# Linear attention laid over chunks: a five-stage order in place of a loop of four passes

## The chip, the cores and the metric

One core of one Trainium2 chip runs the whole kernel in one launch. The engines are TensorE (PE in the rows, PEld its weight loads), VectorE (DVE), ScalarE (ACT), GpSimd (POOL) and SyncE (SP), which issues the DMAs. The metric is the device time of the launch in microseconds, as the median of several runs.

## The reference, cut to what matters

Input x is 4 x 512 tokens of 512 features. It passes four blocks: a linear attention with residual, a routed spline lookup, a differential softmax attention, and a gated feed-forward with Hadamard-mixed weights; the kernel runs the lookup, a norm and the feed-forward around both attentions. The change concerns the part up to the end of the linear attention and its routing:

```python
q = (x @ Wq.T + bq), k = (x @ Wk.T + bk), v = (x @ Wv.T + bv)   # 16 query heads, 8 key heads of 32
q = q * cos + rotate_half(q) * sin                              # the same for k
x = x / max(norm(x), 1e-6); p = x @ R.T                         # per head, R is 16 x 32
feats = concat(sin(p), cos(p)) / sqrt(32)
kv = einsum('bhsf,bhsd->bsfd', kp, v); out = einsum('bhsf,bsfd->bhsd', qp, kv)   # per token, over heads
return out @ Wo.T + bo
# routed lookup: layernorm, signs, scores of 64 tiles, argmax (cluster, then tile),
# min and max of the chosen 8 features over all tokens of a tile, 16-cell piecewise lookup, added to x
```

## The kernel before

The 2048 tokens are four chunks of 512 (NCH = 4), each chunk four tiles of 128 (TPC). Products in 16 bits are made as three (high by high, high by low, low by high: `pairs_product`, L1189), so a 512 x 512 by 128 product is 12 matmuls. TensorE writes PSUM, eight banks of 512 floats (`k.ps`); ScalarE and VectorE take results out. The engines run their own instruction lists and meet through semaphores; on every engine the order is that of the code.

Set-up (`setup_*`, L596 to L954) loads and transposes the weights, mixes the feed-forward weights, and routes all chunks once. Its load order is in `setup_sync`: Wq, x, Wk and Wv, Wo, the four parts of W_down, then eight groups of up and gate weights. Then, for chunk 0, the lookup is applied and its rows are normalized and transposed (L957 to L1169), and the linear attention starts.

A pass `b_*(i, last, next)` (L1209 to L1486) does for chunk i: four value products (taken out at L1411, sent to DRAM and back in another layout by SP, L1380 and L1383); six projections into banks 2 and 3 (L1318), each rotated by a matmul (L1229), multiplied by cosines on GpSimd (L1368) and by sines on VectorE (L1421, L1422), squared on GpSimd (L1372) and summed per head by a matmul (L1234). The inverse lengths come from a square root (L1333) and a reciprocal with one refinement step (L350 to L353). Six products with the random matrix (L1258) are scaled by the spread inverse lengths (L1261, L1330, L1439), reduced to a turn (L1445, L1447), put through Sin (L1340) and split into high and low (L1343, L1451). SP spreads these over 36 transfers (L1391) into `ks` and `qs`. Then 16 pairs of 16-token groups: scores (L1277), mask (L1460), weighted values (L1287), results (L1354, L1485); four output products (L1297), residual (L1475) and bias (L1478). Into the projections of chunk i the routing of chunk i-1 is woven (`last`), between angles and pairs the lookup of chunk i+1 (`next`, L1266 and L1454), and after the pairs its addition, statistics, Sqrt (L1140), rows (L1148) and transposes (L1167). Chunks 1 and 2 run in a hardware loop (`Fori`, L2490), 0 and 3 are written out. After the last chunk its routing stands alone (L2493), then the tile ranges are joined and the lookup and feed-forward phase begins, with its own norm through Ln and Exp (`norm_root_scalar`, L1723).

## Time and profile before

| | us |
|---|---|
| median of 3 runs | 2496.23 (2494.53 to 2498.5) |
| the profiled execution | 2493.57 |
| its span, first to last instruction | 2491.8 |
| TensorE busy | 2077.4 (83%) |
| VectorE busy | 1250.5 (50%) |
| ScalarE busy | 743.3 (30%) |
| GpSimd busy | 200.6 (8%) |

The page cuts the span into 40 slices of 62.3 us and gives the busy share of each engine in tenths, and under PEclk the clock that TensorE was granted, in tenths of full speed (1.0 is 2.4 GHz, 0.5 is 1.2 GHz). A table by stretches gives for each the busy time and instruction count of every engine; a timeline gives instructions in order, with the idle time before them and what ended it in brackets. Matmuls overlap each other, so a mean duration of one is longer than its share of a row of many.

### The profile page before, as it was taken

Reading aid. Unit: us, or ns where it says so; the run is one execution under the profiler, and the core shown is the slowest. Engines: PE = TensorE matmul, PEld = TensorE weight load, DVE = VectorE, ACT = ScalarE, POOL = GpSimd, SP = SyncE. Lnnn points to the kernel's source line nnn. Section 1 sums busy time; section 2 is a strip of 40 time slices with the busy share of each in tenths; the row PEclk is TensorE's granted clock in tenths of the full one; section 3 lists DMA queues with packets and bytes.
Section 4 is the critical chain, followed back from the end, with each engine's and each line's share of the span. In section 5 each row is a group of like instructions: output and inputs, shape, how many; then the busy total and the mean of one; then the engine's idle time right before and its main releaser. Section 6 shows DMA issues by size and latency. Waiting matters only on the chain. (4 is left out here: it accounts for less than half of the span.)

```text
span 2491.8 us, 30544 instructions
## 1 busy us (share of the span) xinstructions
PE 2077.4 (83%) x12014; PEld 981.1 (39%) x12014; DVE 1250.5 (50%) x2301; ACT 743.3 (30%) x1146; POOL 200.6 (8%) x148
## 2 busy tenths in 40 slices
PE   4777477756658548999999999999999999999998
PEld 3444224223223224444444444444444444444443
DVE  4444456364464444645456625662567355633332
ACT  4443131223212312222323522352235223521211
POOL 3340010101002000000000101000100010000000
PEclk8777577767678668999999999999999999999999
DMA  6211420111001311222210211121112111222322
GB/s 255 68 51 17 167 37 22 7 39 17 23 16 17 106 69 62 97 96 85 77 43 29 77 56 35 34 77 51 42 35 77 51 43 34 71 74 100 104 99 87
DMA packets 90978, 158.70 MB, mean 64 GB/s; under 512 B 44182, under 2 KB 55772, under 8 KB 86108
## 3 DMA queue, kind: packets, MB, share of 16 engines
q1 hardware_dynamic: 90844, 156.86, 19.6%
q8 instruction: 91, 1.49, 0.2%
q14 instruction: 43, 0.35, 0.1%
HBM read 128.52 MB, written 18.87 MB: 59 GB/s over the span
## 5 line engine op out<-in xcount | busy, mean ns | idle before, releaser
L1189 PE MATMUL ps<-arena 128*128 128x512 f16 (+1 forms) x4512 | 1006.6, 379 | 30.5 <-DVE arena L1675 12.8
L1189 PEld LDWEIGHTS ps<-arena 128*128 128x128 f16 x4512 | 436.2, 99 | 533.4 <-issue 29.6
L1620 PE MATMUL ps<-arena 128*128 128x512 f16 x1536 | 347.8, 382 | 29.4 <-DVE arena L1666 16.2
L1620 PEld LDWEIGHTS ps<-arena 128*128 128x128 f16 x1536 | 147.2, 98 | 206.7 <-issue 28.1
L1642 ACT ACTIVATE arena<-ps,arena 128x512 f32<-128x512 f32 x128 | 87.7, 685 | 362.4 <-PE ps L1189 362.1
L1675 DVE SCALAR_TENSOR_TENSOR arena<-arena,ps 128x512 f32<-128x512 f32 x128 | 87.8, 686 | 210.2 <-ACT arena L1642 209.5
L2229 ACT ACTIVATE arena<-ps 128x1024 f32<-128x1024 f32 (+3 forms) x128 | 90.2, 705 | 251.9 <-PE ps L2138 251.9
L2334 DVE CAST arena<-arena 128x1024 f16<-128x1024 f32 (+3 forms) x128 | 66.6, 520 | 148.1 <-ACT arena L2229 146.1
L2300 DVE TENSOR_REDUCE arena<-ps 128x2 f32<-128x256 f32 (+3 forms) x128 | 99.5, 819 | 65.1 <-PE ps L2082 65.1
L1684 DVE SCALAR_TENSOR_TENSOR arena<-ps,arena 128x512 f32<-128x512 f32 x128 | 95.7, 748 | 39.8 <-PE ps L1189 39.8
L1703 DVE SCALAR_TENSOR_TENSOR arena<-ps,arena 128x512 f32<-128x512 f32 x64 | 44.0, 687 | 139.7 <-PE ps L1620 139.5
L2336 DVE TENSOR_TENSOR arena<-arena 128x1024 f16<-128x1024 f32 (+3 forms) x128 | 111.4, 870 | 4.4
L2280 POOL TENSOR_TENSOR arena<-arena 128x512 f16<-128x512 f32 x32 | 37.1, 1159 | 742.1 <-ACT arena L2207 742.1
L1666 DVE TENSOR_TENSOR arena<-arena 128x512 f16<-128x512 f32 x128 | 91.6, 715 | 4.0 <-ACT arena L1634 4.0
L1634 ACT ACTIVATE arena<-arena 128x512 f16<-128x512 f32 x128 | 79.7, 622 | 17.5 <-DVE arena L1684 17.5
L685 PE MATMUL ps<-arena 128*128 128x128 f32 x240 | 44.9, 347 | 46.5 <-DVE arena L917 27.5
L728 PE MATMUL ps<-arena 128*128 128x512 f16 x256 | 71.9, 450 | 5.7 <-DVE arena L917 5.7
L1277 PE MATMUL ps<-arena 96*128 96x256 f16 x128 | 29.2, 323 | 54.2 <-issue 32.0
L2136 PE MATMUL ps<-arena 32*128 32x512 f16 (+3 forms) x768 | 72.9, 293 | 0.0
L2204 ACT ACTIVATE arena<-ps 128x512 f32<-128x512 f32 x32 | 19.1, 597 | 166.7 <-PE ps L1189 166.7
L1460 DVE TENSOR_TENSOR arena<-ps,arena 128x256 f32<-128x256 f32 x128 | 47.3, 418 | 38.7 <-PE ps L1277 36.3
L2284 POOL TENSOR_TENSOR arena<-arena 128x512 f32<-128x512 f32 x16 | 18.6, 1163 | 580.2 <-DVE arena L2347 580.2
(266 smaller groups left out, 2442.5 us busy)
## 6 DMA issues: line engine op xcount, KB each, us to landing
arena<-wug_dram SPq DMA_DIRECT2D x128, 512.0 KB, 3.3
arena<-wd_hi_dram SPq DMA_DIRECT2D x16, 1024.0 KB, 5.0
arena<-wd_lo_dram SPq DMA_DIRECT2D x16, 1024.0 KB, 7.2
arena<-arena SPq DMA_DIRECT2D x144, 64.0 KB, 2.1
wug_dram<-arena SPq DMA_DIRECT2D x4, 2048.0 KB, 15.8
arena<-_attn_hidden_states_dram SPq DMA_DIRECT2D x4, 1024.0 KB, 10.4
arena<-in_L_ffn_W_down_dram SPq DMA_DIRECT2D x4, 1024.0 KB, 15.5
arena<-in_L_ffn_W_up_dram SPq DMA_DIRECT2D x8, 512.0 KB, 6.3
```

Of the source, the lines that this page charges most:

```text
L728: ins = pe.matmul(k.ps[:, bank, :], sign, part[:, jc, :], start=(n == 0), stop=(n == 7))
L1189: ins = pe.matmul(out, left[a](c), right[b](c), start=(at == 0), stop=(at == 3 * n - 1))
L1620: ins = pe.matmul(k.ps[:, bank, :], act[x][:, slot, cols], wd[y][:, f, :], start=(f == 0 and m == 0), stop=(f == 7 and m == 2))
L1634: e.activation(k.act_hi[:, g % ACT_SLOTS, :], k.prod[:, g % 2, :], ACT.Copy).then_inc(s["f_hi"], 1)
L1642: e.activation(k.th[:, g % 2, :], k.ps[:, GATE_BANK, :], ACT.Tanh, scale=k.wscale[:, FB + a:FB + a + 1])\
L1666: e.tensor_tensor(k.act_lo[:, g % ACT_SLOTS, :], k.prod[:, g % 2, :], k.act_hi[:, g % ACT_SLOTS, :], ALU.subtract)\
L1675: e.scalar_tensor_tensor(out=th, in0=th, scalar=1.0, in1=k.ps[:, GATE_BANK, :], op0=ALU.add, op1=ALU.mult)\
L1684: e.scalar_tensor_tensor(out=k.prod[:, g % 2, :], in0=k.ps[:, UP_HALF_BANK, :], scalar=k.wscale[:, a:a + 1], in1=th, op0=ALU.mult, op1=ALU ...
L2136: pe.matmul(k.ps[:, bank, queries], x[rows, 4 + b, keys], y[rows, b, queries], start=False, stop=False)
L2229: e.activation(k.p32[:, t % 2, :, queries], k.ps[:, 0:2, queries], ACT.Exp, scale=SCORE).then_inc(s["c_exp"], 1)
L2300: e.tensor_reduce(k.mx[:, u, 4 * b + 2 * j:4 * b + 2 * j + 2], k.ps[:, bank:bank + 2, 0:(u + 1) * P], AXX, ALU.max).then_inc(s["c_max"], 1)
L2336: e.tensor_tensor(k.p_lo[:, t % 2, :, queries], k.p32[:, t % 2, :, queries], k.p_hi[:, t % 2, :, queries], ALU.subtract).then_inc(s["c_p_l ...
```

## The change

The passes become stages -1 to 3, all written out; the hardware loop is gone. In stage i the roles are `now` = i, `new` = i+1, `look` = i+2 and `back` = i-1, where they exist. A stage begins with 17 steps: at step y the scores of pair y and the weighted values of pair y-1 of chunk `now`, and at fixed steps a projection, a rotation or a length of chunk `new` (`QK_AT` = 1, 2, 4, 5, 7, 8; `ROT_AT` = 3, 4, 6, 7, 9, 10; `LENGTH_AT` = 5, 6, 8, 9, 11, 12). On VectorE the token statistics of `back` stand at steps 0, 2 and 4, and the range update of chunk i-2 at step 1. Then the angles of `new` alternate with the output rows of `now` and the lookup of `look`; then the values of `new`, the routing of `back` and the normalization and transposes of `look`. In stage 3 the routing of chunk 2 is in the 17 steps instead.

The bias of the output is added on GpSimd. Square roots with reciprocals become Ln, Exp with factor -0.5, and the same refinement step (`root_refine_vector`), for the lengths, the routing's two deviations and the norm. One bank serves all rotations (4), another all spreads; the lookup's rows are written as cells, slopes and bases into three banks. The buffers of the attention move into the space of the feed-forward weights, after their copy to DRAM is done. SP issues the spread transfers of a chunk first and its values' round trip after them. In the set-up Wk and Wv are loaded before x and taken first, and W_down's parts are loaded one after each of the first four groups. The later lookups read their rows as two halves, by two instructions.

```diff
...
+    k.q2, a = v.at(a, [P, 2, CH], F32)
     k.qr, a = v.at(a, [P, 6, CH], F32)
-    k.q2, a = v.at(a, [P, 2, CH], F32)
-    k.y2, _ = v.at(a, [P, TPC, HID], F32)
-    k.ks, a = v.at(a, [P, 8, CH], F16)
-    k.masked2, _ = v.at(a, [P, 2048], F32)
-    k.ksg, _ = v.at(a, [P, 32, P], F16)
+    k.f_hi, a = v.at(a, [P, 6, CH], F16)
+    k.f_lo, a = v.at(a, [P, 6, CH], F16)
     k.ang, a = v.at(a, [P, 2, CH], F32)
     k.turns, a = v.at(a, [P, 2, CH], F32)
...
+    b = k.wug_at
+    k.qs, b = v.at(b, [P, 16, CH], F16)
+    k.ks, b = v.at(b, [P, 8, CH], F16)
+    k.ksg, b = v.at(b, [P, 32, P], F16)
+    k.ot_hi, b = v.at(b, [P, KC, CH], F16)
+    k.ot_lo, b = v.at(b, [P, KC, CH], F16)
+    k.sm, b = v.at(b, [P, 2, 2, 16, 16], F32)
     k.vr, b = v.at(b, [P, 32, 32], F32)
+    k.y2, b = v.at(b, [P, TPC, HID], F32)
+    k.v0, b = v.at(b, [P, TPC, 256], F32)
...
+def token_root_scalar(k, e, i, n):
+    s = k.s
+    ve, out = k.t4[0], k.t4[1 if n == 1 else 4]
+    done = s["std1" if n == 1 else "std2"]
+    e.wait_ge(s["var1" if n == 1 else "var2"], i + 1)
+    e.activation(out, ve, ACT.Ln).then_inc(done, 1)
+    e.wait_ge(done, 2 * i + 1)
+    e.activation(out, out, ACT.Exp, scale=-0.5).then_inc(done, 1)
...
+    load_nat(1, [(rows_of(d["L0_attn_Wk"]), 2), (rows_of(d["L0_attn_Wv"]), 2)])
     for c in range(NCH):
         sp.dma_start(k.x[:, c * TPC:(c + 1) * TPC, :],
                      d["L0_attn_hidden_states"][c].rearrange("(u p) n -> p u n", p=P)).then_inc(s[f"x_in{c}"], 16)
-    load_nat(1, [(rows_of(d["L0_attn_Wk"]), 2), (rows_of(d["L0_attn_Wv"]), 2)])
     load_nat(2, [(rows_of(d["L0_attn_Wo"])[:, 0:2], 2), (rows_of(d["L0_attn_Wo"])[:, 2:4], 2)])
...
+        if g < 4:
+            sp.dma_start(k.wd_nat[:, g, :], d["L1_ffn_W_down"][g * P:(g + 1) * P, :]).then_inc(s[f"wd_in{g}"], 16)
...
     first(0)
+    first(1)
     setup_stats_vector(k, V)
     setup_scale_vector(k, V)
-    first(1)
+    first(2)
     setup_norm_vector(k, V)
-    first(2)
...
+def b_roles(i):
+    return [n if 0 <= n < NCH else None for n in (i, i + 1, i + 2, i - 1)]
...
+    for bank, n, at in ((LOOK_CELLS, 3, 256), (LOOK_SLOPES, P, 128), (LOOK_BASES, P, 0)):
+        for u in range(TPC):
+            ins = pe.matmul(k.ps[:, bank, u * n:(u + 1) * n], k.oht[:, u * P:(u + 1) * P], k.table[:, at:at + n],
+                            start=True, stop=True)
...
+        if now is not None:
+            if y < PAIRS:
+                score(y)
+            if y:
+                weighted(y - 1)
+        if new is not None:
+            if y in QK_AT:
+                project(QK_AT.index(y))
+            if y in ROT_AT:
+                rotate(ROT_AT.index(y))
+            if y in LENGTH_AT:
+                length(LENGTH_AT.index(y))
...
+    body = back is not None and new is not None
+    if look is not None:
+        pe.wait_ge(s["b_n2"], new + 1)
+        apply_turn_tensor(k, pe, look, 1, LOOK_CELLS)
+    turns(0)
+    output(0)
+    if look is not None:
+        look_rows_tensor(k, pe, look)
+    turns(1)
+    output(1)
+    turns(2)
+    output(2)
+    turns(3)
+    output(3)
+    turns(4)
+    value(0)
+    turns(5)
+    value(1)
+    if body:
+        if look is not None:
+            pe.wait_ge(s["ap_read"], look + 1)
+        route_turn_tensor(k, pe, back, route, 0, BACK_BANK)
+        route_turn_tensor(k, pe, back, route, 1, BACK_BANK)
+    value(2)
+    if body:
+        route_turn_tensor(k, pe, back, route, 2, BACK_BANK)
+        route_turn_tensor(k, pe, back, route, 3, BACK_BANK)
+    value(3)
+    if body:
+        route_key_tensor(k, pe, back, route, BACK_KEY)
+    if look is not None:
+        pe.wait_ge(s["b_spread"], 6 * (new + 1))
+        pe.wait_ge(s["b_y"], 6 * (new + 1))
+        for c in range(KC):
+            if c == 3:
+                pe.wait_ge(s["n_lo"], 2 + KC * look + 1)
+            turn_tensor(k, pe, look, c, NEXT_TURN[c])
+    if body:
+        route_hot_tensor(k, pe, back, route, BACK_BANK[0])
+        for c in range(KC):
+            route_mask_tensor(k, pe, back, route, c, BACK_BANK)
+        route_slice_tensor(k, pe, back, route, BACK_KEY)
...
+    if look is not None:
+        apply_scalar(k, e, look, 1, LOOK_CELLS)
+    for z in range(4):
+        turns(z)
+    keys(0)
+    keys(1)
+    turns(4)
+    keys(2)
+    keys(3)
+    turns(5)
+    if body:
+        route_sign_scalar(k, e, back, route, 0, BACK_BANK)
+        route_sign_scalar(k, e, back, route, 1, BACK_BANK)
+    if body:
+        route_sign_scalar(k, e, back, route, 2, BACK_BANK)
+        route_sign_scalar(k, e, back, route, 3, BACK_BANK)
+    if look is not None:
+        use_log(e)
+        norm_root_scalar(k, e, look)
+        norm_write_scalar(k, e, look, look, k.h, range(TPC), s["n_h"])
+        for c in range(KC):
+            turn_scalar(k, e, look, c, NEXT_TURN[c])
+    if body:
+        route_hot_scalar(k, e, back, route, BACK_BANK[0])
...
+    if now is not None:
+        for u in range(TPC):
+            e.wait_ge(s["b_res"], TPC * now + u + 1)
+            xt = k.x[:, now * TPC + u, :]
+            e.tensor_tensor(xt, xt, k.bo, ALU.add).then_inc(s["b_bo"], 1)
...
+    for y in range(PAIRS + 1):
+        if now is not None:
+            if y < PAIRS:
+                mask(y)
+            if y % 4 == 1 and y > 4:
+                sums(y // 4 - 1)
+        if i >= 2 and y == 1:
+            route_ends_vector(k, V, i - 2, route, BACK_KEY)
+        if new is not None:
+            if y - 1 in ROT_AT:
+                rope(ROT_AT.index(y - 1))
+            if y == SPREAD_AT:
+                lengths()
+            if y == REFINE_AT:
+                refine()
+        if look is not None and y == PAIRS:
+            spline_start_vector(k, V, look)
+        if back is not None:
+            if y == 0:
+                token_sums_vector(k, V, back)
+            if y == 2:
+                token_first_vector(k, V, back)
+            if y == 4:
+                token_second_vector(k, V, back)
+        if i == NCH - 1:
+            if y == 10:
+                route_choice_vector(k, V, back, route, LAST_KEY)
+            if y in (12, 13):
+                route_pick_vector(k, V, back, route, 2 * y - 24, LAST_BANK)
+                route_pick_vector(k, V, back, route, 2 * y - 23, LAST_BANK)
+    body = back is not None and new is not None
+    if now is not None:
+        sums(3)
+    angle(0)
+    if look is not None:
+        spline_place_vector(k, V, look, 1, cells)
+    residual(0)
+    low(0)
+    angle(1)
+    if look is not None:
+        spline_slope_vector(k, V, slopes)
+    residual(1)
+    low(1)
+    angle(2)
+    if look is not None:
+        spline_value_vector(k, V, bases)
+    residual(2)
+    low(2)
+    angle(3)
+    if look is not None:
+        scale_start_vector(k, V, look)
+        scale_tiles_vector(k, V, look, range(TPC))
+    residual(3)
+    low(3)
+    angle(4)
+    value(0)
+    if look is not None:
+        for u in range(TPC):
+            scatter_tile_vector(k, V, u)
+    low(4)
+    angle(5)
+    value(1)
+    if look is not None:
+        add_sum_vector(k, V, look)
+    low(5)
+    if look is not None:
+        norm_sums_vector(k, V, look, range(TPC))
+        norm_spread_vector(k, V)
+    value(2)
+    if look is not None:
+        norm_refine_vector(k, V, look)
+    value(3)
+    if body:
+        route_choice_vector(k, V, back, route, BACK_KEY)
+    if look is not None:
+        for c in range(KC):
+            turn_vector(k, e, look, c, NEXT_TURN[c])
+    if body:
+        for c in range(KC):
+            route_pick_vector(k, V, back, route, c, BACK_BANK)
+    if i == NCH - 1:
+        route_ends_vector(k, V, back, route, LAST_KEY)
...
```

## Rows read from the trace of the kernel before

**Rows 1.** The page, 40 equal slices: TensorE busy and granted clock, in tenths.
```profile
PE   4777477756658548999999999999999999999998
PEclk8777577767678668999999999999999999999999
```
**Rows 2.** Stretches of the span: length, then busy time and count by engine, clock, DMA.
```profile
core 0: us, PE busy (x) PEld busy (x) DVE busy (x) ACT busy (x) POOL busy (x), PEclk, DMA share, GB/s
0.00:265.90 265.90, 181.51 (x843) 111.01 (x843) 117.20 (x237) 110.34 (x171) 74.76 (x36) 0.78 0.31 101
...
300.10:432.40 132.30, 98.12 (x594) 47.00 (x595) 74.12 (x150) 30.78 (x45) 12.58 (x12) 0.78 0.15 29
432.40:596.30 163.90, 101.89 (x610) 48.07 (x609) 83.53 (x181) 39.90 (x61) 12.64 (x12) 0.73 0.11 22
596.30:756.40 160.10, 101.93 (x609) 48.06 (x608) 83.47 (x181) 39.87 (x60) 12.62 (x12) 0.73 0.12 22
756.40:880.80 124.40, 83.24 (x520) 34.57 (x518) 58.20 (x120) 33.89 (x50) 12.62 (x12) 0.75 0.23 59
880.80:915.80 35.00, 16.25 (x78) 11.96 (x78) 12.43 (x42) 9.25 (x15) 0.00 (x0) 0.60 0.00 0
```
**Rows 3.** The same view of the steps of the second pass.
```profile
432.40:473.40 41.00, 31.65 (x128) 11.77 (x126) 14.76 (x38) 13.26 (x21) 12.64 (x12) 0.89 0.19 18
473.40:484.90 11.50, 9.96 (x43) 6.01 (x42) 3.87 (x10) 0.00 (x0) 0.00 (x0) 0.80 0.00 0
484.90:494.60 9.70, 1.94 (x2) 0.50 (x2) 6.06 (x5) 0.63 (x1) 0.00 (x0) 0.50 0.00 0
494.60:516.40 21.80, 11.98 (x13) 3.15 (x12) 14.52 (x25) 12.42 (x19) 0.00 (x0) 0.50 0.17 43
516.40:533.20 16.80, 4.82 (x12) 3.03 (x12) 6.63 (x23) 4.38 (x5) 0.00 (x0) 0.50 0.35 86
533.20:554.60 21.40, 16.39 (x288) 8.49 (x288) 14.55 (x37) 2.39 (x4) 0.00 (x0) 0.85 0.01 2
554.60:565.20 10.60, 10.52 (x48) 4.57 (x48) 9.51 (x15) 0.00 (x0) 0.00 (x0) 1.00 0.01 2
565.20:585.50 20.30, 3.88 (x16) 3.14 (x16) 9.76 (x23) 6.81 (x10) 0.00 (x0) 0.63 0.00 1
```
**Rows 4.** Timeline of the set-up: start, length, engine, line, and idle time before.
```profile
41.52 0.45 PE L685 MATMUL ps<-arena 128*128 128x128 f32 x1 [6.53 <-DMA arena<-in_L_ffn_W_up_dram]
```
**Rows 5.** Timeline of the second pass: a projection at full clock and a rotation.
```profile
460.14 2.76 PE L1189 MATMUL ps<-arena 128*128 128x512 f16 x12
...
462.73 1.02 PE L1229 MATMUL ps<-arena 128*128 128x512 f32 x2
```
**Rows 6.** Groups by line in the second pass: busy, mean ns of one | idle before.
```profile
L1460 DVE TENSOR_TENSOR arena<-ps,arena 128x256 f32<-128x256 f32 x32 | 12.0, 419 | 6.3 <-PE ps L1277 5.2 <-issue 0.5
...
L1439 DVE SCALAR_TENSOR_TENSOR arena<-ps,arena 128x512 f32<-128x512 f32 x6 | 4.1, 685 | 5.2 <-ACT arena L1330 5.2
...
L350 DVE RECIPROCAL arena<-arena 24x512 f32<-24x512 f32 x1 | 3.3, 3341 | 0.9 <-ACT arena L1333 0.9
...
L1445 DVE TENSOR_SCALAR arena<-arena 128x512 f32<-128x512 f32 x6 | 2.9, 487 | 1.3 <-DVE arena L1439 1.2
...
L1478 DVE TENSOR_TENSOR arena<-arena 128x512 f32 x4 | 2.8, 692 | 0.6
```
**Rows 7.** Stretches before the first pass: lookup, addition, statistics to transposes.
```profile
271.90:279.10 7.20, 0.00 (x0) 0.00 (x0) 6.38 (x21) 0.00 (x0) 0.00 (x0) 0.50 1.02 419
279.10:286.50 7.40, 0.00 (x0) 0.00 (x0) 7.21 (x12) 0.00 (x0) 0.00 (x0) 0.50 0.65 265
286.50:300.10 13.60, 3.94 (x16) 3.13 (x16) 6.79 (x19) 5.52 (x9) 0.00 (x0) 0.50 0.00 1
```
**Rows 8.** Timeline of the last routing: the slice of the chosen features.
```profile
904.49 6.99 PE L468 MATMUL ps<-arena 128*128 128x8 f32 x32 [0.78 <-DVE arena L506]
```
**Rows 9.** Timeline of SP's queue in the second pass: the spread transfers.
```profile
506.33 23.30 SPq L1391 DMA_DIRECT2D arena<-arena  x36
```
**Rows 10.** Timeline: the same small VectorE operation beside GpSimd and alone.
```profile
433.28 1.09 POOL L1368 TENSOR_TENSOR arena<-arena 128x512 f32<-128x512 f32 x1 [96.01 <-ACT arena L1318]
433.33 1.08 DVE L374 TENSOR_SCALAR arena<-arena 128x4 f32<-128x4 f32 x1
...
757.08 0.17 DVE L374 TENSOR_SCALAR arena<-arena 128x4 f32<-128x4 f32 x1
```

## What I predict, and how

> **What bounds the kernel now.** I read the page's slices first. TensorE is busy nine tenths or more of each slice from about 950 us on, at full clock; before that it is at four to eight tenths and the clock between 0.5 and 0.8 [rows 1]. The change touches only that first part, so the next view is the table by stage [rows 2]: the set-up up to 265.9 us, the first chunk's lookup and normalization, then four passes of the linear attention (132.3, 163.9, 160.1 and 124.4 us), and a last routing of 35.0. In the second pass TensorE has 101.9 us of work, VectorE 83.5, ScalarE 39.9, GpSimd 12.6: no engine fills its 163.9 us. The third view cuts that pass into its steps [rows 3]. Projections with rotation, squares and the routing of the chunk before take 41.0; the end of the routing and four products with the random matrix 11.5; the square root and reciprocal of the lengths 9.7 with TensorE nearly idle; angles 21.8; lookup 16.8 with TensorE at 4.8; pairs 21.4; output rows 10.6 with VectorE beside it; normalization and transposes 20.3 with TensorE at 3.9; the values are the rest. Each stretch ends with a wait in one chunk's chain while other engines rest. That is what laying chunks over each other can fill.
>
> **The set-up.** The first transpose of an up-projection tile waits 6.5 us for its load [rows 4], behind four 1 MB loads of W_down. The change queues W_down after each of the first four groups, loads Wk and Wv before x, and converts them before the token statistics. x now comes 1 MB later, so the statistics slip while the up tile comes sooner. Bounds 0 and -6.5 us; I take **-4**. The first lookup has narrower result rows in three banks and no half-way stops in its transposes: **-1**, between 0 and -2.
>
> **Old passes, 580.7 us, become five stages (-1 to 3).** A stage has a loop of 17 steps (pairs of chunk i, projections of i+1), a middle (output of i, angles and values of i+1, lookup of i+2) and a tail (normalization of i+2, routing of i-1, in that order on TensorE).
>
> *Loop.* TensorE: six projections of 12 matmuls, 2.76 each when the clock is full, 16.6; six rotations of two passes, 1.02 each, and six lengths of the same size, 12.2 [rows 5]; the pairs at most their 21.4 us window [rows 3], 19.5 without its slow start. Together 48.3. VectorE: 32 masks of 0.42 [rows 6], 13.6 with gaps; four conversions 2.8; six ropes of two operations of 0.69, 8.7; lengths and their refinement 2.8; the token statistics of i-1 another 6; the routing ends of i-2 another 3: 28 to 37, under TensorE's. The last four steps have only pairs and the refinement, 3 us more than TensorE's work; the 3.34 us reciprocal [rows 6] is gone, replaced by an Ln and an Exp on ScalarE, about 0.6 each as an estimate (the square root they stand for was one such operation). I take **53** for stage 0, **55** for 1 and 2. The single rotation bank makes rotation z wait for rope z-1; one round of projection, rotation and length is 4.8 us of TensorE and the rope chain needs 2.5, so the cover holds.
>
> *Middle.* VectorE, in its written order: six angles of three operations (0.69, 0.49, 0.69 [rows 6]), 1.95 each with gaps, 11.7; six low parts 4.3; four residuals 2.9; lookup 7.2 and addition 7.4, by the unrolled first chunk [rows 7]; values and the rest 1.6: **35**. TensorE at full clock: six spreads and six random-matrix products, about 1 us each, 12; output rows 10.5; lookup rows 3.5; two values 2.8: 29. ScalarE 16. VectorE is late. On top: the first lookup rows come behind spread, product and a whole output row (4 us of wait); keys' copies on ScalarE wait for transfers that start after the second low part, 12 issues at 0.6 plus landing (2 us); collisions with GpSimd, below (3 us). **44** for stages 0 and 1. Stage 2 has no lookup: 20 of VectorE, 25.5 of TensorE, with waits **34**. The 2.76 us of twelve matmuls hold only at full clock, and in the old angle window TensorE worked 12.0 of 21.8 us with 24-row matmuls and the clock stayed at 0.50, while the denser pairs window has 0.85 [rows 3]. At half clock TensorE's 29 become 58; I add 3 us to each of the two full middles, to **47**, being nearest the pairs window in density.
>
> *Tail.* From the last low part: statistics 3.1, then table load 1.28, Ln, Exp, refinement 2, four rows 2.9 and 16 transposes at half clock 3.9, as in the 13.6 us that the first chunk took for the same [rows 7]: **12** without routing. In stage 1 the four signs (eight ScalarE operations, 5.6 at an estimated 0.7 each) stand before the table load, and behind the transposes come choice, masks, picks and the 32-matmul slice (7.0 at half clock [rows 8], half of that at full): **25**. Stage 2 has no normalization, only routing: **20**.
>
> Stage sums: stage 0, 53+47+12 = 112; stage 1, 55+47+25 = 127; stage 2, 55+34+20 = 109. Stage -1 has nothing to lay its projections over: 37 for loop and refinement, 36 for angles and lookup (VectorE's 35 less residuals, table load added), 12 tail: 85. Stage 3 is pairs with the routing of chunk 2 woven in, 36, and output rows 13: 49. Each loop begins after a thin tail at half clock: 3 us more in four of them, 12. Sum 112+127+109+85+49+12 = **494 against 580.7, -87**.
>
> *Moved steps.* The bias additions (16 of 0.69 [rows 6]) go to GpSimd at about 1.09, with the routing's statistics waiting for them; covered by the next loop's first pairs, except in the last stage, where the fourth adds 0.4 to a routing that loses as much with its reciprocals. Six rope additions and squares stay where they were. SP's queue now holds the 36 spread transfers ahead of the values' round trip: the 36 need 23.3 us [rows 9] and end before the tail does, but the eight value transfers then wait for the last value row and land about 9 us after it, 1 to 2 us past the shorter tail (in the loop's 53). The ring loads still start well before the last routing ends. The last routing keeps its 35.0 [rows 2]. The three later lookups read split rows, two instructions instead of one: +0.5 at the feed start.
>
> GpSimd: in the trace a four-element VectorE operation beside a GpSimd multiply took 1.08 us and ended with it; its like in the last pass, with GpSimd still, took 0.17 [rows 10]. So one collision costs up to 0.9 us. The Trainium skill, "SBUF — State Buffer", section "Who interferes with whom", states that VectorE instructions with two SBUF inputs or in a two-port mode and GpSimd exclude each other for a whole instruction; by that rule, the trace agrees. Four additions per middle fall beside exactly such operations: 3 us, taken above. The bound for all 16 a stage is the third rival.
>
> **Sum.** Against the profiled execution's 2493.57 us (span 2491.8): -4 -1 -87 +0.5 = **2402**. The median of the three timed runs is 2496.2, 2.7 above the profiled one; half of that offset puts the median at **2403**.
>
> **Rivals.**
> - *Half clock in the middle and tail.* For it: the angle window at 0.50. Against: 3.5 us of every 6 in the new middle are full-array matmuls. Price: 58 instead of 47 twice, 51 instead of 34 in stage 2, 5 more in two tails: +49, so 2452; a half of it, 2428. Chance 0.2, mostly for partial forms.
> - *Everything fills better.* If my extra waits (4+2+3+3 a middle, 12 for loop starts, 5 to 7 in loops) are mostly covered: -35, 2368. Chance 0.15.
> - *Every GpSimd operation collides.* All 16 GpSimd operations hit VectorE at 0.9: 14 a stage, less the 3 taken, in three stages: +33, 2436. Speaking against it is the loop's VectorE slack of 11 us or more. Chance 0.12. The page named above would have it so wherever VectorE is dense with two-operand instructions.
> - *Slower: in-order coupling.* In the loop each engine has two chunks' chains in one order. If the waits for masks and for ropes alternate so that they do not overlap, a loop costs 21.4 plus 41 plus 10 rather than 55 (+17, three times), and if in the middle VectorE and TensorE also take turns, 35+29 rather than 47 (+17, two and a half times), +94 in all: 2497, and with the half clock beside it up to 2540. It decides against the change only from the point where nearly nothing overlaps. Against: double-buffered scores and projection banks. Chance 0.03.
> - *It does nothing*, because transfers end last as before. The old fourth pass waited for them; now a whole tail lies before they are needed. Chance 0.01.
>
> The forecast keeps 0.49. The range leaves out two in ten: **2362 to 2450**. A difference under 0.2% (5 us) can hardly be told from none: faster 0.96, same 0.01, slower 0.03.
>
> **What would show it.** From the first to the last projection-bank eviction the stages should be about 112, 127 and 109 us apart; the loop's TensorE busy over 85% at clock 1.0; VectorE over 75% busy in a middle; the wait for the first lookup rows 4 us; no wait of a score or of the keys' copy for a transfer above 3 us; the stretch from 950 us on unchanged in length. I am wrong if loops take over 62 us or middles over 55; then see whether clock, collisions or mask waits stand before the late operations.

## The result, and the profile after

The changed kernel takes **2407.57 us** (median of 4 runs, 2406.84 to 2411.72) where the kernel before, on the same chip, takes 2496.77 (4 runs, 2494.53 to 2498.5): a ratio of 0.9649, 95% interval 0.9636 to 0.9663. The prediction was 2403, range 2362 to 2450. The profiled execution took 2407.47 us, its span is 2405.7, its mean granted clock 0.903 (before 0.893).

Its page, the same two rows of the 40 slices as [rows 1], now 60.1 us each:

```profile
PE   4777486878877479999999999989998999999998
PEclk7777577988785589999999999999999999999999
```

The thin part ends one slice sooner (slice 15 instead of 16, and the slices are shorter). The steps of the passes, as busy time by stretches with the columns of [rows 2]; each stage has its loop, middle and tail, from the first projection of stage -1 (296.3) to the first statistics of the last routing (790.8):

```profile
core 0: us, PE busy (x) PEld busy (x) DVE busy (x) ACT busy (x) POOL busy (x), PEclk, DMA share, GB/s
296.30:333.90 37.60, 30.12 (x96) 10.06 (x96) 11.00 (x17) 5.38 (x8) 12.57 (x12) 0.86 0.00 0
333.90:376.50 42.60, 38.38 (x100) 17.59 (x100) 29.54 (x62) 18.29 (x25) 0.00 (x0) 0.56 0.15 38
376.50:389.00 12.50, 4.50 (x20) 3.76 (x20) 7.09 (x21) 5.73 (x10) 0.00 (x0) 0.59 0.41 111
389.00:443.60 54.60, 42.52 (x380) 17.67 (x380) 23.98 (x53) 7.79 (x12) 12.58 (x12) 0.93 0.12 10
443.60:488.00 44.40, 38.21 (x148) 17.97 (x148) 32.76 (x66) 18.30 (x25) 5.87 (x4) 0.85 0.15 36
488.00:500.50 12.50, 4.50 (x20) 3.76 (x20) 7.10 (x21) 5.73 (x10) 0.00 (x0) 0.62 0.42 111
500.50:555.80 55.30, 44.19 (x380) 17.88 (x380) 31.37 (x75) 11.20 (x20) 12.58 (x12) 0.87 0.15 9
555.80:599.70 43.90, 36.86 (x148) 17.63 (x148) 32.70 (x66) 18.84 (x27) 5.87 (x4) 0.88 0.15 36
599.70:624.90 25.20, 18.89 (x96) 14.49 (x96) 10.56 (x27) 10.96 (x18) 0.00 (x0) 0.58 0.46 74
624.90:674.50 49.60, 43.99 (x382) 17.95 (x380) 33.49 (x82) 11.20 (x20) 12.59 (x12) 0.94 0.00 1
674.50:710.40 35.90, 31.26 (x116) 14.13 (x116) 21.40 (x32) 17.28 (x24) 4.74 (x4) 0.90 0.18 45
710.40:730.00 19.60, 14.56 (x84) 11.08 (x84) 4.30 (x10) 6.45 (x10) 0.00 (x0) 0.65 0.61 94
730.00:773.00 43.00, 30.88 (x362) 20.20 (x360) 24.22 (x71) 11.46 (x20) 0.00 (x0) 0.58 0.00 1
```

Against the prediction, with its loop starts (3 us each) put into the loops:

| stage | loop | middle | tail | sum predicted | sum measured |
|---|---|---|---|---|---|
| -1 | 37 / 37.6 | 36 / 42.6 | 12 / 12.5 | 85 | 92.7 |
| 0 | 56 / 54.6 | 47 / 44.4 | 12 / 12.5 | 115 | 111.5 |
| 1 | 58 / 55.3 | 47 / 43.9 | 25 / 25.2 | 130 | 124.4 |
| 2 | 58 / 49.6 | 34 / 35.9 | 20 / 19.6 | 112 | 105.1 |
| 3 | 39 / 43.0 | 13 / 17.8 | | 52 | 60.8 |
| all | | | | 494 | 494.5 |

(Predicted / measured, us. Stage 3's "middle" is its output rows, with what follows up to 790.8.) The passes came down from the 580.7 of [rows 2] to 494.5, as forecast to half a microsecond, but with errors of 3.5 to 8.8 us in each stage that cancel. So the agreement of the sum is luck; the experiments have to tell which terms were right.

Around the passes: the set-up ends 4.6 us sooner (261.3 instead of 265.9), from there to the first projection it is 35.0 us instead of 34.2, the last routing and the way to the first feed-forward product take 69.1 instead of 68.3, and the rest 1545.8 instead of 1542.7. So -4.6 +0.8 -86.2 +0.8 +3.1 = -86.1 us of span.

**The waits inside.** TensorE's timeline of the changed kernel at the start of stage 0's loop (start, length, instruction, idle time before it):

```profile
395.96 0.67 PE L1227 MATMUL ps<-arena 128*32 128x64 f32 x16 [7.38 <-DMA arena<-values_dram]
396.56 3.90 PE L1130 MATMUL ps<-arena 128*128 128x512 f16 x12
```

The first weighted values wait 7.4 us for the value transfers (7.5 in stage 1, none in stage 2), and the projection behind them takes 3.90 instead of the 2.76 of [rows 5]: the granted clock was 0.50 from 392.1 to 398.8. SP's queue tells why; its timeline in stage 0:

```profile
464.56 31.04 SPq L1497 DMA_DIRECT2D arena<-arena  x36
495.70 0.53 SPq L1511 DMA_DIRECT2D values_dram<-arena  x1
498.83 4.01 SPq L1515 DMA_DIRECT2D arena<-values_dram  x8
```

The last value row was evicted at 492.8. The 36 spread transfers, 23.3 us in [rows 9], stretch over 31.0 here, because they start behind the second angle's low part and wait for later ones in between; they end at 495.6, so the round trip starts 2.9 us after the last value row. Then come 3.1 us to land in DRAM, 4.0 for eight issues, and the last landing: TensorE goes on at 507.5, 11.8 us after the trip's start.

All engines in stage 0's middle:

```profile
448.77 3.41 PE L1130 MATMUL ps<-arena 128*128 128x512 f16 x12
449.02 0.69 DVE L1565 SCALAR_TENSOR_TENSOR arena<-ps,arena 128x512 f32<-128x512 f32 x1 [4.62 <-PE ps L1263]
449.74 0.49 DVE L1569 TENSOR_SCALAR arena<-arena 128x512 f32<-128x512 f32 x1
...
452.11 2.94 PE L1192 MATMUL ps<-arena 64*128 64x3 f32 x24
...
455.09 0.17 DVE L1070 COPY arena<-ps 128x12 f32<-128x12 f32 x1 [4.13 <-PE ps L1192]
...
458.68 1.47 POOL L1484 TENSOR_TENSOR arena<-arena 128x512 f32<-128x512 f32 x1 [21.96 <-DVE arena L1585]
...
459.84 0.60 DVE L1569 TENSOR_SCALAR arena<-arena 128x512 f32<-128x512 f32 x1
...
474.34 2.00 ACT L1413 ACTIVATE arena<-arena 96x1024 f16<-96x1024 f16 x2 [1.02 <-DMA arena<-arena]
...
476.25 0.57 ACT L1401 ACTIVATE arena<-ps 128x512 f32<-128x512 f32 x1
476.87 1.59 PE L1260 MATMUL ps<-arena 24*128 24x512 f32 x2 [4.31 <-ACT arena L1401]
```

VectorE waits 4.62 us for the first angle's products, 4.13 for the first lookup rows (4 forecast), and once more behind the key copies, which keep ScalarE from the spread's eviction (L1401); TensorE stands 4.31 us there. Beside a GpSimd addition the same VectorE operation takes 0.60 instead of 0.49 us, and the addition 1.47 instead of 1.09. The clock was at its lower level twice in this middle, for its first 6.5 us and for 6.8 us behind the pause:

```profile
443.60:450.00 6.40, 6.06 (x11) 2.14 (x12) 1.74 (x4) 2.47 (x3) 0.00 (x0) 0.50 0.00 0
477.40:484.20 6.80, 6.80 (x23) 3.47 (x22) 6.47 (x12) 3.73 (x5) 0.00 (x0) 0.50 0.42 104
```

### The profile page after: what moved, and what is told of

It reads as the page before. It is cut to its first block and busy times, and to the rows that moved or that the text cites. A ratio compares the mean times of both kernels' runs of the same rounds, so it can differ in the third digit from the quotient of the medians.

```text
span 2405.7 us, 29600 instructions
## 1 busy us (share of the span) xinstructions
PE 2087.0 (87%) x12078; PEld 996.0 (41%) x12078; DVE 1228.1 (51%) x2281; ACT 749.2 (31%) x1163; POOL 221.2 (9%) x164
## 5 line engine op out<-in xcount | busy, mean ns | idle before, releaser
L1130 PE MATMUL ps<-arena 128*128 128x512 f16 (+1 forms) x4512 | 1019.1, 381 | 19.8 <-DVE arena L1893 12.9
L1529 DVE TENSOR_TENSOR arena<-ps,arena 128x256 f32<-128x256 f32 x128 | 47.8, 418 | 100.9 <-PE ps L1214 100.9
L1755 PE MATMUL ps<-arena 128*128 128x128 f32 x192 | 33.6, 335 | 67.0 <-ACT arena L1970 67.0
L719 PE MATMUL ps<-arena 128*128 128x128 f32 x240 | 43.8, 341 | 43.0 <-DVE arena L951 30.2
## 6 DMA issues: line engine op xcount, KB each, us to landing
arena<-_attn_hidden_states_dram SPq DMA_DIRECT2D x4, 1024.0 KB, 11.8
```

What stands on the lines that cost most here:

```text
L1130: ins = pe.matmul(out, left[a](c), right[b](c), start=(at == 0), stop=(at == 3 * n - 1))
```

## Experiments

Each kernel has 4 runs; medians and ranges are given. "Feed start" is the start of the first feed-forward product in the profiled execution: 949.1 us before, **859.9** in the changed kernel. It leaves out what varies behind it, but it is read from one execution of each kernel. All are the changed kernel with one edit, unless said otherwise.

Two things limit small differences. The variants ran on three other chips, where the kernel before took 2494.0 to 2496.3 us instead of 2496.8, so medians carry up to 3 us of the chip. And the profiled execution of the changed kernel starts stage 0's projections 11.5 us after the first mask, where seven variants that keep the loop's order took 13.3 to 14.4: about 2 us of what a variant pays at its feed start are not its edit's.

### Two projections ahead of the first weighted values (project_first)

```diff
-QK_AT = (1, 2, 4, 5, 7, 8)
-ROT_AT = (3, 4, 6, 7, 9, 10)
-LENGTH_AT = (5, 6, 8, 9, 11, 12)
+QK_AT = (0, 1, 3, 4, 6, 7)
+ROT_AT = (2, 3, 5, 6, 8, 9)
+LENGTH_AT = (4, 5, 7, 8, 10, 11)
...
                 score(y)
+        if new is not None and y in QK_AT:
+            project(QK_AT.index(y))
```

> The changed kernel with every projection, rotation and length one step earlier in the loop, and the projection of a step ahead of the step's weighted values, so that two projections stand before the first weighted values. In the changed kernel TensorE stood still 7.4 and 7.5 us there in stages 0 and 1, waiting for the value transfers; I had counted 1 to 2. If that wait is on the path, two projections at about half clock, some 9 us, fill it, and the second of them ends about 6 us sooner in both stages: 12 us less, a median of about 2396. The rival: the rotation chain on VectorE and GpSimd sets the length of the loop; then the loops keep their 54.6 and 55.3 us and the median stays within 3 us of 2407.6.

Measured: 2394.62 (2393.48 to 2397.81), feed start 845.6, so 13 and 14.3 less. TensorE's timeline in stage 0, and the loop by stretches:

```profile
388.27 4.48 PE L1130 MATMUL ps<-arena 128*128 128x512 f16 x12 [0.99 <-DVE arena L1771]
...
392.81 2.76 PE L1130 MATMUL ps<-arena 128*128 128x512 f16 x12
395.91 0.66 PE L1227 MATMUL ps<-arena 128*32 128x64 f32 x16 [0.34 <-DMA arena<-values_dram]
```

```profile
388.10:437.10 49.00, 44.64 (x382) 18.36 (x382) 23.42 (x51) 7.70 (x12) 12.60 (x12) 0.93 0.13 11
```

The weighted values still start at 395.9, when the transfers have landed, but two projections are done. From first mask to the end of the refinement the loops shrink by 4.9, 5.8 and 1.2 us. The wait was on the path; the rotation chain does not set the loop.

### The key copies out of the angles (keys_late)

```diff
-    keys(0)
-    keys(1)
     turns(4)
-    keys(2)
-    keys(3)
     turns(5)
...
         norm_write_scalar(k, e, look, look, k.h, range(TPC), s["n_h"])
+    keys(0)
...
+        if y in (0, 2, 3):
+            keys((0, 2, 3).index(y) + 1)
```

> The changed kernel with ScalarE's four copies of the keys taken out from between its angle steps: the first stands behind the normalization, the other three in the next loop. In the changed kernel VectorE waited 2.2, 1.3, 0.6 and 3.0 us for the spread copy that stands behind the first two key copies in stages -1 to 2. If this queueing is all that they cost, 5 us less (3 to 8), median 2402.5. The rival: TensorE's pause of 4.3 us in front of the fifth spread also costs it the clock (0.50 in the 5 us after it), so that values and the next angles come out sooner too: 10 us less, 2397.5. Third: the copies delay the projections' evictions in the loop and it comes to nothing, 2407.

Measured: 2393.92 (2391.66 to 2397.33), feed start 849.6: 13.7 less by the median, 10.3 at the feed start. The fifth spread now stands so:

```profile
473.94 1.12 PE L1260 MATMUL ps<-arena 24*128 24x512 f32 x2 [1.29 <-ACT arena L1401]
```

1.29 us of pause instead of 4.31, and full speed (1.12) instead of 1.59. From refinement to last low part the middles lose 2.4, 1.1, 0.8 and 3.8 us, 8.1 in all. VectorE's waits for that eviction in the changed kernel sum to 2.2 + 1.3 + 0.6 + 4.8 = 8.9, of which my text had counted only the longer one of stage 2. So the queue by itself accounts for the middles. The total is nearer the rival's 10 us than the 5 expected. The second half-clock stretch of the changed kernel's stage 0 is gone, but no run separates what it adds from the queue. Of the gain in span, 2.8 us lie behind the feed start and are not the edit's (last section).

### The bias additions back on VectorE (bias_vector)

```diff
-            e.tensor_tensor(xt, xt, k.bo, ALU.add).then_inc(s["b_bo"], 1)
...
+        e.wait_ge(s["b_res"], TPC * now + u + 1)
+        e.tensor_tensor(xt, xt, k.bo, ALU.add).then_inc(s["b_bo"], 1)
```

(taken out of `b_pool`, put into `residual` of `b_vector`)

> The changed kernel with the sixteen bias additions on VectorE, right behind the residual, instead of on GpSimd. My prediction had 3 us of collisions with them in each middle, 0.9 us for each. By that the middles gain 3 and lose 4 additions of 0.73, 2.9: no difference, median 2407 to 2408. The rival, from the trace of the changed kernel: beside the GpSimd addition VectorE's operations took 0.60 instead of 0.49 us, 0.1 us for each, while the GpSimd addition itself grew from 1.09 to 1.47; then moving them costs 2.9 less 0.4 in three middles, 7 to 8 us more, median 2415.

Measured: 2412.75 (2410.64 to 2414.93), feed start 862.7: 5.2 and 2.8 more. Its middle in stage 0:

```profile
445.70:491.70 46.00, 38.63 (x148) 17.91 (x148) 35.15 (x71) 18.31 (x25) 0.00 (x0) 0.85 0.14 35
```

The full middles grow by 1.6 and 1.8 us, VectorE's busy time by 2.4. With 3 us of collisions they would have stayed level. So a middle paid about 0.4 us for the overlap (four operations, 0.1 each), not 3; GpSimd, which has time, pays the rest. Stage 2's middle grows by 1.0, but it varies by more than that without an edit (last section). The growth lies nearer the rival, below its 2.5 a middle; that a part of the additions finds gaps is my reading. By the ratios to the kernel before on the same chip (0.9675 against 0.9649) the kernel lost some 6.5 us, again near the rival's 7 to 8.

### The lookup's rows ahead of the output row (rows_first)

```diff
     turns(0)
-    output(0)
     if look is not None:
+        if now is not None:
+            pe.wait_ge(s["b_ot_lo"], TPC * (now + 1))
         look_rows_tensor(k, pe, look)
+    output(0)
```

> The changed kernel with the lookup's rows ahead of the first output row on TensorE (behind it before). VectorE waited 4.1 and 4.4 us for them in stages 0 and 1, as I had counted (4). If VectorE sets the middle, as predicted, the rows come 3.4 us sooner and so does everything behind them: 7 us less, median 2400.5. The rival: TensorE, busy 38 of the middle's 44 us, sets it, and the change of order gains nothing: 2407, or a little more because the rows run at half clock.

Measured: 2414.06 (2408.45 to 2415.01), feed start 865.7: 6.5 and 5.8 **more**. The main expectation missed the sign; the rival had allowed for "a little more", for the reason that the trace shows. TensorE's timeline in stage 0's middle:

```profile
450.24 5.49 PE L1192 MATMUL ps<-arena 64*128 64x3 f32 x24
...
455.66 4.82 PE L1130 MATMUL ps<-arena 128*128 128x512 f16 x12
```

The middle starts at 0.50. In the changed kernel the output row comes first, reaches full clock within its 3.41 us, and the 24 small matmuls behind it take 2.94. Here they take 5.49 at half clock, and the output row behind them 4.82: 10.1 us for the pair instead of 6.2, so the second spread starts 3.6 us later, counted from the last refinement operation, while the rows are read only 1.1 us sooner. The middles of stages 0 and 1 grow by 1.4 each. The rest of the 5.8 us stands where the edit changes nothing: 2.1 at stage 0's value wait and 1.6 in stage 2's middle, which has no lookup. So the order itself is worth about 3 us here, not 6.

### The loop's halves, and the middle's, one after the other (loop_apart, middle_apart)

```diff
     for y in range(PAIRS + 1):
...
+    for y in range(PAIRS + 1):
         if new is not None:
             if y in QK_AT:
```

(on TensorE, ScalarE and VectorE alike)

> The changed kernel with the loop's two halves one after the other on every engine: first the sixteen pairs of one chunk, then the projections, rotations and lengths of the next. By my prediction a loop overlaps 21.4 us of pairs with 37.6 us (measured in stage -1 for projections to refinement), so that it grows from 54.6 to 66 us in stages 0 and 1 and from 49.6 to 59 in stage 2: 32 us more, median 2440. The rival is that the loop was only as long as the sum of its TensorE work with its wait, and the halves overlap little in fact: up to 5 us more, median under 2413. A second rival: the pairs alone run at half clock too, 25 us more in all three on top, 2465.

Measured: 2425.87 (2422.25 to 2428.63), feed start 880.4: 18.3 and 20.5 more. Stage 0's pairs, then its projections to the refinement:

```profile
389.30:412.50 23.20, 14.21 (x264) 7.42 (x268) 12.88 (x36) 1.80 (x3) 0.00 (x0) 0.78 0.36 24
412.50:448.30 35.80, 29.02 (x128) 10.09 (x117) 11.42 (x18) 5.98 (x9) 12.57 (x12) 0.94 0.00 0
```

The loops grow by 5.1, 3.8 and 8.3 us, less than the 11.4 I expected: the pairs take 23.2 with most of an 8.7 us wait for the values in it, some 15 without, and the projections to the refinement 35.8. TensorE is busy 43.2 us in the two together and 42.5 in the woven loop, so the work is the same; what the weaving filled is some 5 us in the two loops that wait for the values either way, and 8.3 in stage 2, which does not.

```diff
-    turns(0)
     output(0)
     if look is not None:
         look_rows_tensor(k, pe, look)
-    turns(1)
     output(1)
-    turns(2)
     output(2)
-    turns(3)
     output(3)
+    turns(0)
+    turns(1)
+    turns(2)
+    turns(3)
     turns(4)
```

(VectorE likewise: residuals with the lookup, then the angles with the addition)

> The changed kernel with the middle's parts one after the other: the output rows with the lookup first, then all six angles with the addition. If weaving them pays as I predicted (VectorE at work all through), the stretches add up as in the kernel before: output and lookup 16 us, angles 22 to 25 at half clock, addition and values 7 to 8: 46 to 50 instead of 44.4 and 43.9, 4 us more in each of two stages and 1 in stage 2: median 2417. By the in-order rival of my prediction they would hardly overlap already, and nothing changes: 2405 to 2409. A third possibility, from the run with the rows first: four output rows in a row bring the clock up before the lookup rows and keep it for the first angles; then 3 us less in each, 2399.

Measured: 2429.52 (2427.76 to 2431.27), feed start 882.3: 22 more by both. Stage 0's output rows with the lookup, then its angles:

```profile
447.60:469.80 22.20, 19.85 (x84) 9.16 (x84) 12.32 (x31) 3.83 (x6) 4.74 (x4) 0.92 0.00 0
469.80:497.50 27.70, 23.20 (x64) 9.58 (x64) 20.51 (x35) 14.23 (x20) 0.00 (x0) 0.64 0.24 58
```

The middles grow by 5.5, 4.8 and 9.4 us, and stage -1's, which has no output rows, by 3.4. In the angle stretch TensorE is at 0.64: between the spreads and products nothing dense stands any more. Stage 2, which has no lookup to fill the angles, loses most; I had given it 1 us. The in-order rival (nothing overlaps anyway) falls in both runs.

### The set-up's order (setup_old, setup_undo)

> The changed kernel with the set-up's old order: x ahead of Wk and Wv, the four parts of W_down ahead of the first up-projection tile, and the statistics ahead of the second group's conversion. I predicted 4 us for this part; the trace of the changed kernel ends its set-up 4.6 us sooner (261.3 instead of 265.9). If that comes from the order of the loads, the 6.5 us wait for the up-projection tile is back and the median is 2412. The rival: it comes from elsewhere (other table loads, other waits of the routing), and the set-up ends as it does now: 2407.6.

The kernel moved the loads alone (x ahead of Wk and Wv, W_down's parts ahead of the first tile), and not the engines' order that the text names. Measured: 2421.38 (2418.49 to 2423.73); the set-up ends at 273.8, 12.5 later. VectorE converts Wk and Wv first and now waits for them behind x, so statistics and tile come late together. The two edits belong together. The full undo puts the statistics ahead of the second conversion on VectorE and ScalarE as well:

```diff
     first(0)
-    first(1)
     setup_stats_vector(k, V)
     setup_scale_vector(k, V)
-    first(2)
+    first(1)
     setup_norm_vector(k, V)
+    first(2)
```

> The changed kernel with the set-up's old order in all its parts: the loads as in setup_old, and on VectorE and ScalarE the statistics ahead of the second group's conversion. (The kernel setup_old moved only the loads and left the two engines' order as changed, other than its text says; its set-up ended at 273.8 us.) If the order is all of the set-up's gain, it ends at 265.9 us as in the kernel before, 4.6 later than in the changed kernel, median 2412. The rival: the old order alone doesn't bring the 265.9 back, because the 4.6 us came from other edits, and the set-up ends near 261.

Measured: 2412.97 (2407.65 to 2416.61), feed start 867.3, set-up end 267.2. The wait of [rows 4] is back:

```profile
41.33 1.94 PE L719 MATMUL ps<-arena 128*128 128x128 f32 x8 [6.23 <-DMA arena<-in_L_ffn_W_up_dram]
```

The order is the cause of the 4.6 us (5.9 here).

### The reciprocal of the lengths (reciprocal)

```diff
-        ... ACT.Exp, scale=-0.5)
+        ... ACT.Exp, scale=0.5)
...
+        V.link(e.reciprocal(r0, r0))
```

> The changed kernel with the reciprocal of the lengths back on VectorE: ScalarE's Exp gets the factor +0.5 and gives the root, and VectorE takes 3.34 us (its row of before) for the reciprocal ahead of the refinement. By my prediction it stood on the path, between the last length and the first spread: 3.4 us more in each of four stages, 13 to 14 us, median 2421. The rival: the last weighted values and the one-hot transposes cover it in stages 0 to 2, and only stage -1 pays: 3 to 5 us, 2412.

Measured: 2425.46 (2421.38 to 2429.28), feed start 881.4: 17.9 and 21.5 more. VectorE's timeline in stage 0:

```profile
448.74 3.34 DVE L1555 RECIPROCAL arena<-arena 24x512 f32<-24x512 f32 x1
452.12 0.68 DVE L1556 TENSOR_TENSOR arena<-arena 24x512 f32<-24x512 f32 x1
```

From first projection eviction to refinement every stage grows by 3.3 or 3.4 us, 13.5 in all: nothing covers it. Another 1.4 is a later set-up end. The rest of the 21.5 is 2.5 at the start of stage 0's loop, where the value wait varies, and 1.1 and 2.8 in the middles of stages 0 and 2; I have not traced it further.

### Taking the waits out together (best, second, no_early)

The version `best` moves the four value products into steps 12 to 15 of the loop (banks 2 and 3), their transfers ahead of the spread transfers, the key copies as above, the slice of a routing into step 1 of the next loop, and the lookup forward:

```diff
+VALUE_AT = (12, 13, 14, 15)
...
+            if y in VALUE_AT:
+                value(VALUE_AT.index(y))
+            if look is not None and y == REFINE_AT:
+                pe.wait_ge(s["b_n2"], new + 1)
+                apply_turn_tensor(k, pe, look, 1, LOOK_CELLS)
...
+    look_rows_tensor(k, pe, look, True)
     turns(0)
     output(0)
-    look_rows_tensor(k, pe, look)
+    look_rows_tensor(k, pe, look, False)
```

(True: cells and slopes; False: bases. VectorE takes every lookup step one angle sooner and the norm's sums behind the last angle.) `second` has the slice at step 3 instead, `no_early` is `second` without the lookup part.

> A version that takes what the first runs showed: the values' products stand in the last steps of the loop and their transfers ahead of the spread transfers on SP; the key copies as in keys_late; the slice of a routing moves into the next loop; the lookup's one-hot transposes stand in the loop, its cells and slopes ahead of the first spread, its bases behind the first output row, and VectorE takes place, slope, value, scale, scatter and addition one angle sooner. If the waits add up: 13 us for the value transfers, 11 for the keys, 6 in each of three middles for the lookup, 7 for slices at full clock, 4 for values out of the tail: 50 us less, median 2357. The rival: with rows ahead of the dense output rows the clock is late, as in rows_first, and half of it is lost: 2382.

Measured: **2372.73** (2367.78 to 2374.98), ratio to before 0.9511 (0.9494 to 0.9528), feed start 819.9. That is 35 us under the changed kernel, between the two expectations. Stage 0's loop and middle:

```profile
380.50:430.20 49.70, 46.02 (x415) 21.84 (x416) 24.16 (x54) 9.38 (x14) 12.59 (x12) 1.00 0.01 2
430.20:469.30 39.10, 30.45 (x116) 12.12 (x113) 34.94 (x70) 14.86 (x22) 5.88 (x4) 0.81 0.38 68
```

The loop is TensorE's (93% busy, clock 1.00), the middle VectorE's (89%). Now the picture is the one that I had predicted for the change itself. The lookup's small matmuls stand ahead of the output row here too, but behind a dense loop at clock 1.00: sixteen of them take 2.02 us, so the loss of rows_first does not come back.

```profile
431.32 2.02 PE L1194 MATMUL ps<-arena 64*128 64x3 f32 x16 [0.20 <-ACT arena L1017]
```

> The version best with the slice of a routing two steps later in the next loop, at step 3 behind two projections, and its range update at step 4. In best the slice stood at the start of stages 2 and 3, took 7.0 us there at half clock, and put off the first projection: from the first mask to the first projection eviction stage 2 took 12.7 us, stage 0 4.3. If the slice runs at full clock behind the projections, 3.5 us, stage 2 gains about 5 and stage 3 little, whose pairs are waits anyway: 5 to 7 us less than best, median 2366. The rival: stages 2 and 3 are set by VectorE or by the pairs, and it changes nothing, 2372.7.

Measured: 2376.27 (2370.9 to 2381.23), feed start 827.0: no faster than `best`. From first mask to first mask stage 2 gains 1.8 us (99.9 instead of 101.7), not 5, and from stage 3's first mask to the feed start it is 137.7 instead of 132.3, 5.4 more. The later range update comes ahead of the token rows of the next chunk's routing, in stage 3 on its critical side: a delay moved, not removed. (That it is this wait is read from the order in the code, not tested.) The middles of stages 0 and 1, which the edit leaves alone, are 1.7 and 1.5 us longer than in `best`: so much two executions can differ.

> The version second without its lookup part: the one-hot transposes, the lookup's rows and VectorE's order in the middle stand as in the changed kernel, only the values, the key copies and the slice are moved. It tells what VectorE's waits for the first angle and the first rows are worth (4.6 and 4.1 us in stage 0 of the changed kernel, the prediction's 4 us a middle). If VectorE sets the middle, as I predicted, both waits are paid in full in the two full middles and in part in stage -1: 15 us more than second, near 2381. If TensorE sets it, which worked 38 of its 44 us, 5 us more at most, 2371.

Measured: 2383.37 (2378.62 to 2388.5), feed start 839.2, of which 2.4 stem from the set-up: about 10 us of the passes against `second`, 7 by the medians. From refinement to the next first mask, stage -1 is 1.4 us shorter without the lookup part, stage 0 1.8 and stage 1 4.5 longer. Stage 0's middle is even shorter, by 0.7 (counted from the refinement's end, 40.0 against 40.7); only its tail is longer (12.5 against 10.0), because the norm's sums are back in it. VectorE's two early waits are back as well, 2.3 + 3.5 us in stage 0 and 3.6 + 5.5 in stage 1 (the last one below), and yet those middles change by -0.7 and +4.3: the waits are worth far less than their length. Of the two bounds in my text neither is met: 10 us lie midway between TensorE's 5 and VectorE's 15, the 7 of the medians nearer TensorE's, and the ranges of the two kernels overlap. A middle that is 38 of 44 us busy on one engine and 33 on the other is, as I read it, bound by neither alone.

```profile
550.72 0.17 DVE L1070 COPY arena<-ps 128x12 f32<-128x12 f32 x1 [5.54 <-PE ps L1193]
```

## Why the prediction held, and where not

The mechanism held: chunks that fill each other's waits, worth 86.2 us in the passes against 87 forecast. That the two agree to a microsecond is luck, for each stage missed by 3.5 to 8.8. Which engine sets a stretch I had too simply: in the changed kernel TensorE is busy for 78% of a loop, with a value wait in it, and VectorE for 74% of a middle. The undo runs put rough sizes to the parts: by the feed start 20.5 for weaving the loop, 22.4 for the middle and 2.8 for GpSimd's additions, each with 1 to 3 us of stage 0's longer value wait in it, and 13.5 by the stages for the reciprocals of the lengths. That is 59 of 86; the remaining 27 (routing of the chunk before beside other work, the unrolled loop, the norm behind the angles) I have not taken apart, and undos need not add up.

- *Set-up, -4 within 0 to -6.5:* -4.6, and its cause is shown. (In kernels with this set-up it ended between 259.6 and 262.7.)
- *First lookup, -1:* +0.8, outside its bounds of 0 to -2. The transposes without a stop gave what I said, but 24 narrow matmul instructions (twelve products, two for each) cost more than eight of 259 columns. The step that failed is "narrower result rows" as a gain. The kernel before, then the changed one:

```profile
268.04 3.82 PE L976 MATMUL ps<-arena 64*128 64x259 f32 x8 [0.68 <-ACT arena L983]
...
263.44 5.49 PE L1192 MATMUL ps<-arena 64*128 64x3 f32 x24 [0.68 <-ACT arena L1017]
```

- *Loops:* 56, 58, 58 forecast, 54.6, 55.3, 49.6 measured. Right by accident. TensorE's sum of 48.3 looks good beside loops 0 and 1 without their value waits, 47.2 and 47.8, but its own work in them was 42.5 and 44.2: projections, rotations and lengths came as summed (29.0 in loop_apart, 28.8 forecast), the pairs took 14.2 there instead of 19.5. And "1 to 2 us past the shorter tail" was 7.4 and 7.5, because I let the round trip start at the last value row although I had written that the 36 spread transfers stand ahead of it; their queue ended 2.9 us later, and the trip itself took 11.8 us where I had 9. The 3 us for the last four steps and the extras for stages 1 and 2 made up for it. Stage 2, with no wait (the slice of its tail covers it), shows the surplus: 8 us too many.
- *Middles:* 47, 47, 34 against 44.4, 43.9, 35.9. The 4 us for the lookup rows came as 4.1 and 4.4. The 3 for collisions were 0.4: [rows 10] show a four-element operation that ends with a GpSimd multiply, and I carried its 0.9 over to each of four additions. But the addition starts 0.16 us into a low part (458.52 to 459.20), and it is the addition that is stretched, by 0.38; the angle's first operation behind it reads PSUM and takes its usual 0.68; only the next one, from 459.84, meets the addition's last 0.3 us and loses 0.1. So the third rival (every GpSimd operation collides, +33) falls too. The Trainium skill, "SBUF — State Buffer", section "Who interferes with whom", leaves out of the exclusion VectorE instructions with at most one SBUF input, outside the two-port modes, and gives the ports to whichever of the two issues first; the trace agrees in kind with both. I had read the exclusion and not its exceptions. Not in my sum were the 4.6 us ahead of the first angle.
- *Half clock:* VectorE 74% busy in a middle, TensorE 86%, at 0.85. The first 6.5 us run at 0.50, and again 6.8 us behind the key copies. In each TensorE lost about 3 us of its work, an estimate from the rows (2.07 instead of 1.12 for a spread or a product, 3.41 instead of 2.75 for an output row); how much of it the middle paid, and so whether my 3 us were right, no run separates. A full half-clock middle (rival one) appeared only in stage -1, which has no output rows: 42.6 instead of 36, the largest miss of a middle. There VectorE's list was the wrong bound. At 0.56 TensorE is busy 38.4 of 42.6 us, each spread and each product taking 2.07.
- *Stage 3:* 52 against 60.8. Pairs with the routing woven in took 43.0 at clock 0.58 instead of 39, and the range update of chunk 2 stands ahead of the last routing's sums with 3.4 us that I had not counted.
- *Tails:* 12, 25, 20 against 12.5, 25.2, 19.6.
- *Last routing and feed start:* 69.1 instead of 68.3, as forecast within 0.3.
- *The stretch from 950 us on unchanged:* 3.1 us longer; see the last section.

Of the marks under "what would show it": the stages are 112.1 and 118.8 us apart at their first projection evictions and the third 105.1 at its masks (112, 127, 109 said); the lookup wait is 4.1 to 4.4; the keys' copies wait 0.4 to 1.9 us for transfers; VectorE is at 74%, just under its 75; and the loop's TensorE share is 78% at 0.93 instead of over 85% at 1.0. That last mark is the one that shows the value wait, and I had no mark for the weighted values themselves.

## What to carry to other kernels

When independent chains are laid over each other, go through each queue with the new order and date its last entry, not its length: here a round trip behind 36 transfers held TensorE for 15 us, of which two moved projections gained 13 back. After the change, look for the engine that is idle at the start of each stretch, and for the copy that stands ahead of someone else's eviction; moves of this kind, together, gave another 35 us. And put dense matmuls, not small ones, first behind a thin stretch: here the two steps took 6.2 us in one order and 10.1 in the other, of which the middle paid 1.4. A sum that comes out right shows little: compare it stage by stage.

## What the hardware showed that I had not expected

The stretch behind the feed start has the same instructions in all these kernels. It took 1542.7 us before and 1543.0 in keys_late, but 1545.7 to 1547.5 in the changed kernel and all other variants. One place where the 3 us arise, the same 6 us of work before (first) and after (second):

```profile
1442.00:1448.00 6.00, 6.00 (x28) 3.05 (x27) 0.12 (x1) 0.00 (x0) 0.00 (x0) 0.81 0.00 0
```

```profile
1352.70:1358.70 6.00, 6.00 (x21) 2.97 (x20) 0.12 (x1) 0.00 (x0) 0.00 (x0) 0.56 0.00 0
```

In the 6 us ahead of both TensorE was busy 2.2 us; in one execution the clock came back with 0.81 on average, in the other with 0.56, which is 28 against 21 matmuls done. A second such place, some 200 us later, makes the other half. So differences of up to 3 us between two such kernels may be the clock's and not the edit's. Why it falls one way or the other here I can't say.

Second, the same value transfers let stage 0 start its projections 11.5 to 14.4 us after its first mask, from kernel to kernel, with nothing changed ahead of them in the queue; the changed kernel's profiled execution has the 11.5. And the middle of stage 2 took 34.7 to 38.8 us in variants that leave it alone, 35.9 in the changed kernel. I have not found why.
